# Building the experts' row lists from marks on TensorE, and storing and loading expert rows in pairs

## The reference, cut to what matters

```python
xn = layernorm(x)
agg = segment_sum(xn[dst] * edge_weight[:, None], src, 6250)     # rows of xn gathered, weighted, summed
gnn = relu((xn + agg) @ W1 + b1) @ W2 + b2
x   = x + gnn + mix(xn)                       # mix: eight heads, a 32x32 matrix each, summed over all rows
xn2 = layernorm(x)
vals, idx = top_k(xn2 @ gate_w + gate_b, 2)   # two experts for each row
p   = softmax(vals)
moe = sum_k p[k] * (relu(xn2 @ w1[idx[k]] + b1[idx[k]]) @ w2[idx[k]] + b2[idx[k]])
out = x + layernorm(xn2 + moe) * gamma + beta
```

## Time and profile before

| | before |
|---|---|
| median of 3 runs | 2534.15 us (2533.29 to 2534.36) |
| profiled execution | 2535.64 us |
| its span, first to last instruction | 2533.9 us |
| mean granted TensorE clock | 0.831 |
| busy: PE, DVE, ACT, POOL | 1644.0, 1426.9, 624.4, 1650.6 us |
| moved by DMA | 346.60 MB |

### The profile page before, as it was taken

One profiled execution on the slowest core, in us unless ns is written; L12 is line 12 of the kernel. 1 busy time (PEld: TensorE's weight loads), 2 busy tenths in 40 slices (PEclk: granted clock), 3 DMA queues, 4 the chain that ended last, 5 costly groups with the idle time before them and its releaser, 6 DMA issues. The chain is left out here.

```text
span 2533.9 us, 38997 instructions
## 1 busy us (share of the span) xinstructions
PE 1644.0 (65%) x8994; PEld 1376.4 (54%) x8995; DVE 1426.9 (56%) x4047; ACT 624.4 (25%) x1879; POOL 1650.6 (65%) x1773
## 2 busy tenths in 40 slices
PE   5504656661555688876777777776638999999500
PEld 2204655661444577755555556565537888888500
DVE  8599656552776666665555555555333443444377
ACT  4704665550000022211111111111113333333100
POOL 8003888886787677777777777777624554555575
PEclk9856777775777799998888898889769999999855
DMA  9999991005333244433433334333663111111355
GB/s 302 346 346 342 323 317 36 17 17 70 121 115 122 86 126 124 127 117 116 117 112 116 116 114 117 117 113 117 108 220 125 62 62 58 62 61 62 104 184 158
DMA packets 241682, 346.60 MB, mean 137 GB/s; under 512 B 36023, under 2 KB 194927, under 8 KB 241566
## 3 DMA queue, kind: packets, MB, share of 16 engines
q0 software_dynamic: 67072, 164.59, 22.6%
q1 hardware_dynamic: 153854, 161.25, 20.1%
q10 hardware_dynamic: 20640, 19.41, 2.4%
HBM read 183.09 MB, written 162.05 MB: 136 GB/s over the span
## 5 line engine op out<-in xcount | busy, mean ns | idle before, releaser
L1265 POOL DMA_INDIRECT lower<-xn_rows,lower x816 | 817.7, 1002 | 263.3 <-issue 230.2
L609 POOL DMA_INDIRECT edge_records_sorted<-lower x224 | 311.0, 1388 | 233.6 <-ACT lower L720 165.7
L1304 PE MATMUL bank<-lower 128*128 x912 | 326.7, 443 | 207.8 <-SPq L1159 184.1
L1440 DVE TENSOR_TENSOR xh<-xh,bank 128x256 f32 x456 | 190.1, 417 | 354.2 <-PE bank L1305 353.4
L1423 DVE TENSOR_SCALAR lower<-iota_n,lower 128x128 f32<-128x128 f32 x912 | 281.8, 362 | 66.9 <-issue 51.8
L1304 PEld LDWEIGHTS bank<-lower 128*128 128x128 f32 x912 | 164.5, 210 | 277.4 <-issue 267.7
L653 PE MATMUL bank<-lower 128*64 128x128 f32 x1568 | 228.1, 319 | 123.4 <-ACT lower L704 120.8
L1305 PE MATMUL bank<-lower 128*128 x912 | 301.8, 416 | 0.0
L653 PEld LDWEIGHTS bank<-lower 128*64 128x64 f32 x1568 | 221.9, 167 | 128.1 <-DVE lower L920 121.5
L1809 POOL DMA_INDIRECT expert_rows<-arena,dest_idx x114 | 113.7, 997 | 206.4 <-DVE arena L1904 196.0
L1895 DVE TENSOR_SCALAR arena<-bank,b_tile 128x128 f32<-128x128 f32 x456 | 128.4, 344 | 174.7 <-PE bank L1838 174.7
(11 more groups left out here) (318 smaller groups left out, 2457.9 us busy)
## 6 DMA issues: line engine op xcount, KB each, us to landing
rows_by_expert<-upper SPq DMA_DIRECT2D x32, 3456.0 KB, 25.8
lower<-xn_rows,lower POOLq DMA_INDIRECT x816, 2.8
lower<-in_L_ffn_w SPq DMA_DIRECT2D x16, 512.0 KB, 10.4
upper<-in_L_ffn_w SPq DMA_DIRECT2D x16, 512.0 KB, 10.4
xn_rows<-xh SPq DMA_DIRECT2D x7, 896.0 KB, 5.1
arena<-xn_rows ACTq DMA_DIRECT2D x7, 896.0 KB, 5.4
lower<-xn_rows ACTq DMA_DIRECT2D x49, 128.0 KB
x_plus_beta<-lower ACTq DMA_DIRECT2D x49, 128.0 KB
```

Of the source, the lines that this page charges most:

```text
L609: pool.indirect_dma_start(rec_dram, bass.IndirectOffsetOnAxis(quad_idx[i][:, c:c + 1], 0), quads[i][:, c * QW:(c + 1) * QW], None).then_in ...
L1265: pool.indirect_dma_start(edge_rows[:, t % ROUND, :], None, xn_dram, bass.IndirectOffsetOnAxis(source.bitcast(U32)[:, t:t + 1], 0)).then_i ...
L1304: pe.matmul(sums_at(u), edge_sel[:, 2 * u % ESEL, :], rows_flat[:, ds(at, D)], start=True, stop=False)
L1440: dve.tensor_tensor(xh[:, at], xh[:, at], sums_at(u), ALU.add).then_inc(s_acc, 1)
```

## The change

- **Clearing.** disp_dram and its 32 stores of zeros are gone.
- **Dispatch.** POOL's dispatch(s) with its two scatters a tile is gone. ACT stores a tile's xn2 rows once, plainly, at their own rows of the new xn2_dram (in keep). XB goes from 12 to 3.
- **Marks.** placed(s) keeps the rank within the expert's list as an integer and splits off its low seven bits. ACT's new mark(s), two parts after the rank, writes for each of the two choices two 128x128 matrices in bf16 into the residual's words of that tile, which are used up by then: with gap = (column - low)^2, relu(partition - partition * gap) is the partition number where the column is the row's low place, and zero elsewhere; relu(a - a * gap) with a = 2 * tile + choice + 1 is the tile and choice in the same way.
- **Lists.** In the set-up, DVE makes for each of the 98 columns the one-hot matrix of the list's tile (high places, 128x114 in bf16, seven operations over 14 columns each), and PE sums, over the 98 columns, marks times one-hot: 196 matmuls into two banks, one giving the partition and one the tile and choice for each entry of each list. From these DVE makes the row to gather and the row to scatter to (2 * row + choice; entries that stand for nothing go to spare rows).
- **Experts.** Gathers read xn2_dram by these lists; scatters write the pair rows of y_dram, so that the two results of a row lie beside each other.
- **Last stage.** SP loads a group's pairs plainly, 2 KB for each row, up to three groups ahead; POOL has nothing to do there. SP's order of loads and stores is written out anew.
- **Weights.** w2 of the first four experts waits until the lists have read the marks that lie under it; w1 is loaded as before.

```diff
-    XB, XD = 12, 4
+    XB = 3
...
-    disp_dram = nc.dram_tensor("rows_by_expert", [NBLK * P, D], F32).ap()
-    y_dram = nc.dram_tensor("expert_rows", [XT * P, D], F32).ap()
+    xn2_dram = nc.dram_tensor("xn2_rows", [NTP, D], F32).ap()
+    y_dram = nc.dram_tensor("expert_rows", [TOPK * NTP + XT * P + 1, D], F32).ap()
...
-                sp.wait_ge(s_zero, 2)
-                each = NBLK // NFILL
-                for k in range(NFILL):
-                    sp.dma_start(disp_dram[k * each * P:(k + 1) * each * P, :].rearrange("(p n) d -> p n d", p=P),
-                                 no_row.unsqueeze(1).to_broadcast([P, each, D])).then_inc(s_cleared, 16)
...
-                pool.iota(expert_at[:], pattern=[[NTP, NX]], base=0, channel_multiplier=0,
-                          allow_small_or_imprecise_dtypes=True).then_inc(s_consts, 1)
...
                     act.activation(xh[:, at], xn2[s % XB], ACT.Copy).then_inc(s_xn2k, 1)
+                    act.dma_start(xn2_dram[ds(bucket_now[s] * P, P), :], xn2[s % XB]).then_inc(s_xn2st, 16)
                     act.wait_ge(s_x2b, s + 1)
                     act.dma_start(x2b_dram[:, at], x2b).then_inc(s_x2st, 16)
+
+                def mark(s):
+                    act.wait_ge(s_low, s + 1)
+                    for k in range(TOPK):
+                        at, j = bucket_now[s] * (2 * D) + k * (2 * P), s * TOPK + k
+                        if j >= 2:
+                            act.wait_ge(s_list, j - 1)
+                        act.activation(low_gap[j % 2], iota_n[:], ACT.Square, bias=low_minus[s % 2][:, k:k + 1]).then_inc(s_lowgap, 1)
+                        act.wait_ge(s_lowgap, j + 1)
+                        act.activation(marks[:, ds(at, P)], low_gap[j % 2], ACT.Relu, bias=iota_pc[:, 0:1], scale=partition_minus)
+                        act.activation(marks[:, ds(at + P, P)], low_gap[j % 2], ACT.Relu, bias=tile_plus[:, j:j + 1],
+                                       scale=tile_minus[:, j:j + 1]).then_inc(s_list, 1)
 
                 for c, h, n in CHUNKS:
                     act.wait_ge(s_turn, BT + BC + 2 * c + h + 1)
...
+                    if u - 2 in rank_unit:
+                        mark(rank_unit.index(u - 2))
...
-                def dispatch(s):
-                    pool.wait_ge(s_slot, s + 1)
-                    if s >= XD:
-                        pool.wait_ge(s_disp[s % XD], 16 * TOPK * (s // XD))
-                    pool.sem_inc(s_apart, 1)
-                    for c in range(s * TOPK, s * TOPK + TOPK):
-                        pool.indirect_dma_start(disp_dram, bass.IndirectOffsetOnAxis(slot_all[:, c:c + 1], 0),
-                                                xn2[s % XB], None).then_inc(s_disp[s % XD], 16)
-
                 pool.wait_ge(s_dec, 1)
                 for k in range(EP):
                     pair(k)
-                    for s in range(NT):
-                        if scatter_pair[s] == k:
-                            dispatch(s)
...
-                        dve.wait_ge(s_disp[s % XD], 16 * TOPK * ((s - XB) // XD + 1))
+                        dve.wait_ge(s_xn2st, 16 * (s - XB + 1))
...
+                    chosen = expert_all[:, ds(b * TOPK, TOPK)]
+                    then(dve.tensor_copy(chosen, idx8[:, 0:TOPK]))
+                    dve.tensor_tensor(past_all[:, ds(b * (TOPK * (NX - 1)), TOPK * (NX - 1))].rearrange("p (k e) -> p k e", k=TOPK),
+                                      chosen.unsqueeze(2).to_broadcast([P, TOPK, NX - 1]),
+                                      iota_n[:, 0:NX - 1].unsqueeze(1).to_broadcast([P, TOPK, NX - 1]), ALU.is_gt).then_inc(s_dve, 1)
+                    n.add()
+                    then(dve.tensor_tensor(hot[s % 2], chosen.unsqueeze(2).to_broadcast([P, TOPK, NX]),
...
-                    dve.tensor_tensor(place, ranks_at, expert_at[:], ALU.add).then_inc(s_place, 1)
+                    dve.tensor_tensor(hot_place, hot[s % 2], ranks_at.unsqueeze(1).to_broadcast([P, TOPK, NX]),
+                                      ALU.mult).then_inc(s_place, 1)
                     dve.tensor_tensor(hot_sum, hot_sum, hot_both[s % 2], ALU.add).then_inc(s_hsum, 1)
                     dve.wait_ge(s_place, s + 1)
-                    then(dve.tensor_tensor(hot_place, hot[s % 2], place.unsqueeze(1).to_broadcast([P, TOPK, NX]), ALU.mult))
                     dve.sem_inc(s_apart, 1)
-                    then(dve.tensor_reduce(slot2[:], hot_place, AX, ALU.add))
-                    dve.tensor_copy(slot_node[:, ds(bucket_now[s] * TOPK, TOPK)], slot2[:]).then_inc(s_dve, 1)
-                    n.add()
-                    dve.tensor_copy(slot_all[:, s * TOPK:(s + 1) * TOPK], slot2[:]).then_inc(s_slot, 1)
-                    dve.wait_ge(s_slot, s + 1)
+                    then(dve.tensor_reduce(rank2[:], hot_place, AX, ALU.add))
+                    ranks_i = rank_all[:, ds(bucket_now[s] * TOPK, TOPK)]
+                    then(dve.tensor_copy(ranks_i, rank2[:]))
+                    then(dve.tensor_scalar(low_i, ranks_i, P - 1, None, ALU.bitwise_and))
+                    if s >= 2:
+                        dve.wait_ge(s_lowgap, TOPK * (s - 1))
+                    dve.tensor_scalar(low_minus[s % 2], low_i, -1.0, None, ALU.mult).then_inc(s_low, 1)
+                    dve.wait_ge(s_low, s + 1)
...
-                    load_weights(sp, e)
+                    sp.dma_start(w1_sb[:, e], w1[e].rearrange("(c p) f -> p c f", p=P)).then_inc(s_we[e], 16)
+                for e in range(WAHEAD):
+                    last = min(NT, -(-(e + 1) * FC * D // D))
+                    sp.wait_ge(s_lists, TOPK * last)
+                    sp.dma_start(w2_sb[:, e], w2[e].rearrange("(m p) d -> p m d", p=P)).then_inc(s_we[e], 16)
...
+                pe.wait_ge(s_wide, 1)
+                pe.matmul(bank[0][:, 0:P], expert_wide, ident[:], start=True, stop=True).then_inc(s_row, 1)
+                for j in range(NJ):
+                    if j % LCOLS == 0:
+                        pe.wait_ge(s_high, j // LCOLS + 1)
+                    at = 2 * j * P
+                    pe.matmul(bank[4][:, 0:XT], marks[:, at:at + P], high_hot[:, j, :], start=j == 0, stop=j == NJ - 1)
+                    pe.matmul(bank[5][:, 0:XT], marks[:, at + P:at + 2 * P], high_hot[:, j, :],
+                              start=j == 0, stop=j == NJ - 1).then_inc(s_lists, 1)
...
+                by_expert = lambda a: a.rearrange("p (j e) -> p j e", e=NX - 1)
+                dve.tensor_tensor(by_expert(past_base), by_expert(past_all),
+                                  tiles_f[:, 0:NX - 1].unsqueeze(1).to_broadcast([P, NJ, NX - 1]), ALU.mult).then_inc(s_dve, 1)
...
+                dve.tensor_tensor(high, high_i, base_of, ALU.add).then_inc(s_dve, 1)
...
+                for j in range(0, NJ, LCOLS):
+                    dve.tensor_tensor(high_hot[:, j:j + LCOLS, :], high[:, j:j + LCOLS].unsqueeze(2).to_broadcast([P, LCOLS, XT]),
+                                      iota_n[:, 0:XT].unsqueeze(1).to_broadcast([P, LCOLS, XT]), ALU.is_equal).then_inc(s_high, 1)
...
-                dve.tensor_tensor(past_slot, past_slot, tile_step.unsqueeze(1).to_broadcast([P, NJ, NX - 1]),
-                                  ALU.mult).then_inc(s_dve, 1)
...
+                dve.wait_ge(s_lists, NJ)
+                dve.wait_ge(s_rows, 1)
+                listed, marked = bank[4][:, 0:XT], bank[5][:, 0:XT]
+                dve.tensor_scalar(mark_i, marked, -1.0, 0.0, ALU.add, ALU.max).then_inc(s_dve, 1)
+                dve.scalar_tensor_tensor(spare_at, marked, 0.0, spare_row, ALU.is_equal, ALU.mult).then_inc(s_dve, 1)
+                dve.wait_ge(s_dve, n.add(2))
+                dve.tensor_scalar(tile_i3, mark_i, 1, None, ALU.arith_shift_right).then_inc(s_dve, 1)
+                dve.tensor_scalar(plane_i, mark_i, 1, None, ALU.bitwise_and).then_inc(s_dve, 1)
+                dve.wait_ge(s_dve, n.add(2))
+                dve.scalar_tensor_tensor(rows_all[:], tile_i3, float(P), listed, ALU.mult, ALU.add).then_inc(s_rows, 1)
+                dve.wait_ge(s_rows, 2)
+                dve.scalar_tensor_tensor(dest_all, rows_all[:], float(TOPK), plane_i, ALU.mult, ALU.add).then_inc(s_dve, 1)
+                dve.wait_ge(s_dve, n.add())
+                dve.tensor_tensor(dest_all, dest_all, spare_at, ALU.max).then_inc(s_rows, 1)
...
-                        pool.sem_inc(s_apart, 1)
-                        pool.tensor_copy(dest_idx[p][:], own_rows[:, ds(t, 1)]).then_inc(s_ydi[p], 1)
+                        pool.tensor_copy(dest_idx[p][:], dest_all[:, ds(t, 1)]).then_inc(s_ydi[p], 1)
...
-                        pool.indirect_dma_start(tok[p], None, disp_dram,
+                        pool.indirect_dma_start(tok[p], None, xn2_dram,
...
-            def _(pool):
-                for i, (t0, k0, m) in enumerate(GROUPS):
-                    if i >= FROWS:
-                        pool.wait_ge(s_frow[i % FROWS], rows_landed(i - FROWS))
-                    pool.sem_inc(s_apart, 1)
```

(49 more changed lines are left out.)

147 lines of the change are left out of this document (64 added, 83 removed).

## The result

The changed kernel takes 2441.32 us (median of 4 runs, 2438.21 to 2446.2), the kernel before 2534.26 beside it (2533.29 to 2535.76): ratio 0.9635, 95% interval 0.9618 to 0.9651. It is 93 us faster; the forecast was 2416, with a range from 2396 to 2450.

A forecast was written before the change was run, and what follows sets the result against it. POOL's issue was taken to bound the last stage and the pass after 1090 us, PE the dense tiles before. Terms -3 - 96 + 0 + 11 + 0 - 30 = -118 from 2535.6 gave 2417.6, as median 2416; range 2396 to 2450.

The forecast's parts named there:

- the last stage bound by DMA: Rival, last stage: one queue keeps 177 GB/s, 25.7 MB take 145 us, no gain there; 2446 us, chance 0.09.
- Clearing, -3: Sort before the pass: without the 32 stores of zeros POOL's scatters there run slightly faster; -3 us, at most 6.
- Scatters, -78: Pass after 1090 us: 60 dispatch scatters leave POOL's order, 1.3 us each; -78 us.
- the lead, -23: Dense tiles before 1090 us: without 22 scatters POOL's gathers get 11 pairs ahead, not 2; saves 23 us afterwards.
- Marks and VectorE in the dense tiles, +5: First 17 tiles: 4 turns late by up to 0.9 us behind the marks, plus some VectorE work; +5 us, bounds 0 to 20.
- End of the pass, 0: After the last gather: late stage_h and marks take about as long as the last two scatters; 0, bounds -4 and +5.
- Set-up, +11: Set-up before the experts: list operations and 196 matmuls make it 21.8 to 28.2 us against 12; +11 us taken.
- Experts, 0 with bounds -3 and +4: Expert stage: gathers and scatters still move 128 rows of 1 KB each, so no change in time.
- Last stage, -30: Last stage: without POOL's gathers, VectorE's 101.6 us set it, 116 us against 145.8; -30 us, bounds -32 and -20.
- VectorE holding POOL's issue: Rival, pass: three added VectorE operations a tile hold POOL fully, 16 us over 32 tiles; 2432 us, chance 0.08.
- The marks hold PE at every tile: Rival, pass: each turn late by 3.4 us, none absorbed, 167 us; 2578 us, slower, chance 0.04.
- PE's chain: Rival: PE's own work and stalls set the whole pass, perhaps 40 of 96 us remain gained; 2472 us, chance 0.12.

The follow-up runs named there:

- e9: The changed kernel run again without edits, as control beside e10 and e11: 2447.37 us, ratio 0.9633 to the kernel before.
- e10: The changed kernel with the marks moved directly ahead of relu and the lists' empty entries reading 128 different rows: 2427.23 us, ratio 0.9561.
- e11: e10 with three more small VectorE copies in each tile's placing, each waiting for the one before: 2444.28 us, one run.
- e4: The changed kernel with the 32 clearing stores and 98 scatters put back beside the new work: 2784.64 us, one run; kernel before there 2839.35.
- e12: e10 with the placing's last four VectorE operations spread around the next two parts' sums: 2649.08 us, ratio 0.9286; kernel before there 2856.02.
- e8: The changed kernel with e10's two edits and six more activations a tile in the marks: 2671.37 us, one run; kernel before there 2851.44.

## Why the prediction was right, and where its sum was off

The way the time was gained is the forecast's: POOL's scatters and the last stage's gathers go, and the two stretches that they filled get shorter by about what was worked out. The size is in part luck. 2441 lies 5 us above 2436, the end of the forecast's own bounds. The stated range reaches it only because it takes in a rival, the last stage bound by DMA (2446), and that rival did not come.

**Clearing, -3.** -2.7 in the first profile; but e9, e10 and e11, without the clearing too, have the first gather at 627.9, 629.2 and 626.4, and the kernel before has it at 628.6. In its own group e4, with the clearing back, has it at 638.9 against 634.6 to 635.5 in the three runs without. A few us are possible, but no run sets them apart from the 3 us by which kernels that are equal up to there differ; the bound 0 to -6 holds.

**Scatters, -78, and the lead, -23.** Right in mechanism, by the count of POOL's instructions. From the last gather ahead of part 168 to the last of all, POOL issued 568 (60 of them scatters) in 720.7 us before, 492 in 629.5 us after, and 492 in 625.6 us in e10: 1.27, 1.28 and 1.27 us each. Fewer instructions at the same pace are the gain. e4 does not confirm it, since there POOL did not set the pace. In size it is -91.1 in place of -101. Behind part 168 there were 58 scatters, not 60 (75 us); at part 168 POOL had issued 324 gathers in place of 308, so 8 pairs of lead and not 9 (20 us); and some 4 us went back into waits for places. The forecast named those waits as what would show it wrong, and they are there, behind part 168 (the line of "issue" is the 0.3 us between two gathers; the 48 waits hold 14 us of that kind too):

```profile
POOL lower L1276 <- issue: 135.6, 444, 0.6
POOL lower L1276 <- SPq L1147: 21.7, 48, 4.9
```

That TensorE would follow came true, but not by its clock: the forecast let the granted clock rise from 0.87 towards 0.96 in the second half, and it fell to 0.83 (0.91 in e10).

**Marks and VectorE in the dense tiles, +5: the step that failed.** They cost 16.8. The forecast took four turns late by up to 0.9 us from the trace of before, and little for VectorE. In their place the turns wait five times for stage_h, 11.0 us in all and up to 6.8, and the gate sums wait for keep. TensorE's waits for both in parts 84 to 168, after:

```profile
PE bank L1331 <- ACT lower L1196: 11.0, 5, 6.8
PE bank L1368 <- ACT lower L1220: 7.1, 6, 3.7
```

and before:

```profile
PE bank L1334 <- ACT lower L1203: 4.0, 1, 4.0
PE bank L1371 <- ACT lower L1227: 3.6, 5, 1.0
```

That is 10.5 us more in all. Two things were not priced. The marks begin when VectorE's placing ends, so every microsecond there moves them and what stands behind them. And in some dense tiles they stand ahead of keep and not of stage_h. e10 gives 7.6 us back when the marks move: keep's wait falls to 3.3 us, but stage_h's only to 9.4. e11, one run, shows that three small operations in the placing cost about 1 us a tile. The 9.1 us that e10 still loses (218.5 against 209.4 before) stay open. They would fit the operations that the change adds on VectorE, which e12 leaves unsettled; and by e8 activations are not free at the marks' new place in these tiles either. The three buffers for xn2 in place of twelve were not what cost it: VectorE's normalization (L1598), which waits for their stores, shows no idle time ahead of it. The 2 us ahead of part 84 stay open too.

**End of the pass, 0.** -1.2. It is likely the sum of two effects: e10's end is 6.3 us shorter than the control's, so the marks' old place cost about as much there as the last scatters had.

**Set-up, +11.** +9.7, by the lower branch: VectorE's seven batches set the pace, TensorE keeps up behind them. The first list matmul starts 6.8 us into the stage (6.9 forecast) and the last at 18.6 (18.7; with six batches of 1.8 us the forecast's 17.3 should have been 17.7). Neither the upper branch, 28.2 us, nor the estimate of 25.9 us came.

```profile
L1744 DVE TENSOR_TENSOR lower<-lower,iota_n 128x1596 bf16<-128x1596 f32 x7 | 12.2, 1812 | 0.0
L1709 PE MATMUL bank<-lower,upper 128*128 128x114 bf16 x98 | 11.7, 228 | 1.1 <-DVE lower L1744 0.9
```

**Experts, 0 with bounds -3 and +4: failed.** +9.4, and 0 once the empty entries read different rows (510.9 in e10, 510.9 before). The step took "128 rows of 1 KB each as now" for the same work. The trace has the landing of every second tile's gather: 3.3 us in tile 42, 3.1 to 3.6 in tiles 76, 78, 80 and 84, 3.6 to 3.9 from 104 on, 2.6 to 2.8 in all others behind tile 8. Those are the tiles in which many or all entries stand for nothing (XT is the most that the lists can need), and all such entries read row 0: by the reference, with its default inputs, 31 of the 128 entries are filled in tile 42, 22, 17, 2 and 59 in the next four, 16 in 104, none from 105 on, and 118 or more in every other tile whose landing is known behind tile 8. In e10 all of them land after 2.6 to 2.8 us. The first gather of the stage lands 1 us later than before (7.4 us against 6.4), in e10 too (7.3); its cause stays open.

**Last stage, -30.** -32.4: VectorE waits once, for the first rows, and not again.

```profile
DVE upper L2008 <- DMA lower<-in_L_ffn_gamma: 11.9, 1, 11.9
```

**The rivals.** DMA as the last stage's bound falls: 224 GB/s at a share of 0.66 went beside a VectorE busy for 100.5 of 116 us. VectorE holding POOL's issue falls: gathers behind part 168 average 472.05/492 = 0.96 us, as before. "The marks hold PE at every tile" had the mechanism right (29 waits behind part 168, 99.5 us, up to 6.1 us each) and the price wrong: there the wait took the place of the wait for rows, as the forecast had said of the later tiles, and cost 4 us of the second half (e10). PE's chain did not set the second half: POOL kept its pace of 1.27 to 1.28 us an instruction, with the turns' waits and, in e10, nearly without them.

## What to carry to other kernels

In an engine that runs in order, look not at how long the new work takes but at what stands behind it and at what it waits for: work that waits for a late input belongs behind whatever is due earlier, here ahead of a step with three parts of room. A wait is priced by the wait that it replaces, so find the stretches in which the waiting engine has none to give; here the dense tiles, where three copies of 0.19 us cost about 1 us a tile. And when work is put back as a test, look whether its time comes back by the path that was claimed: in e4 the size was right and the path was not. Last, fill the empty entries of an index list with different rows.

## What the runs showed of the hardware

A gather of 128 rows whose indices all name the same 1 KB row landed after 3.6 to 3.9 us, one of 128 different rows after 2.6 to 2.8, at the same issue time on POOL (0.96 us). Lists filled in part lay between or at the lower end of that: in the changed kernel and its repeat e9, 3.1 and 3.2 us with 69 of 128 entries on that row, 3.3 and 3.6 with 97. In a stage with little slack for landing that was 9 us.

TensorE's list matmuls (114 columns in bf16, a weight load each) began 94 ns apart at a granted clock of 0.5 (1.2 GHz), and, while they ran on without a pause, went over to 52 ns each at 1.0 (2.4 GHz), 93 in 4.86 us of busy time, with VectorE still feeding them:

```profile
1793.00:1798.00 5.00, 5.00 (x81) 5.00 (x79) 5.00 (x4) 0.00 (x0) 0.00 (x0) 0.77 0.43 128
1798.00:1803.00 5.00, 4.86 (x93) 4.54 (x91) 5.00 (x6) 0.23 (x1) 0.00 (x0) 1.00 0.86 290
```

The Trainium skill (TensorE: Matmul & The Clock Gate, Back-to-back issue gap) gives 81 ns for a pair at 128 columns, sustained; this trace shows less at 114, and the measurement decides.
